# Third layer's edge loop: the 128 x 1024 destination compare as eight 128 x 128 compares with a per-partition scalar, in the accumulating form

## What is computed

```python
# h = relu(layernorm(x)); id_Xe = (src, dst)
features = H[id_Xe[0]]                               # a row per edge, by source node
M_in = concatenate([features, Xe], axis=1)           # Xe: 64 attributes per edge
Y = relu(M_in @ M_W.T + M_b)
Z = segment_sum(Y, id_Xe[1], num_segments=6250)      # sum over the edges of a destination
H_next = relu(concatenate([H, Z], axis=1) @ U_W.T + U_b)
x = x + H_next
```

## Time and profile before

| | |
|---|---|
| Time, median of 3 runs | 8234.38 us (8220.6 to 8267.23) |
| Profiled execution: span from first to last instruction | 6576.8 us |
| Profiled execution: its own time with what lies around the span | not recorded; the median less the span is 1657.6 us |
| PE, DVE, ACT, POOL busy, share of the span | 76%, 46%, 27%, 59% |
| The edge loop of the third layer, first to last gather issue on POOL | 3865.4 to 5915.4 us |
| In it: PE, DVE, ACT, POOL busy, of 2065 us | 1634, 360, 531, 1572 us |

### The profile page before, as it was taken

The page is one execution under the profiler, slowest core; times in us unless marked ns, Lnnn a source line. Parts: engine busy times, 40 slices in busy tenths (PEclk is TensorE's granted clock), DMA queues, the critical chain, the costliest instruction groups (busy, mean ns, idle before and its releaser), DMA issues. The chain is left out here.

```text
span 6576.8 us, 115590 instructions
## 1 busy us (share of the span) xinstructions
PE 5007.3 (76%) x35178; PEld 4266.4 (65%) x35178; DVE 3022.6 (46%) x3931; ACT 1799.8 (27%) x3844; POOL 3882.2 (59%) x3427
## 2 busy tenths in 40 slices
PE   2338888888888888841999957877878787771898
PEld 2315665665566655531999957777777777771898
DVE  7757777777777777746322131111111111113322
ACT  0024555555555545510000012222222222220000
POOL 5748788888788888750000047777777777773000
PEclk9668888888888888955999955555555555555898
DMA  9335555555555555522999846666666666652895
GB/s 358 77 84 141 151 153 152 143 150 150 154 155 146 150 149 154 153 61 84 329 366 366 312 128 202 204 203 203 205 204 203 206 204 197 202 178 62 336 389 215
DMA packets 659138, 1262.13 MB, mean 192 GB/s; under 512 B 167881, under 2 KB 467466, under 8 KB 633268
## 3 DMA queue, kind: packets, MB, share of 16 engines
q1 hardware_dynamic: 381076, 726.95, 32.8%
q10 hardware_dynamic: 168480, 416.21, 18.9%
q0 software_dynamic: 109184, 115.05, 9.8%
HBM read 924.66 MB, written 490.51 MB: 215 GB/s over the span
## 5 line engine op out<-in xcount | busy, mean ns | idle before, releaser
L696 POOL DMA_INDIRECT att_gl<-tab_l,att_ix x1568 | 1933.5, 1233 | 487.6 <-issue 472.3
L1184 POOL DMA_INDIRECT sum_gl<-tab_l,sum_ixs x1568 | 1572.3, 1003 | 524.7 <-issue 477.8
L937 ACT ACTIVATE att_acc<-att_pc 128x392 bf16<-128x392 f32 x2352 | 1083.3, 497 | 1324.1 <-PE att_pc L715 1122.6
L712 PE MATMUL att_pc<-att_ohl,att_ohv 128*128 128x392 bf16 x2352 | 863.0, 367 | 272.0 <-DVE att_ohl L812 271.7
L1134 PE MATMUL sum_pm<-sum_msg,sum_S 128*128 128x64 f32 x3136 | 680.0, 407 | 425.6 <-ACT sum_msg L1158 425.5
L1134 PEld LDWEIGHTS sum_pm<-sum_msg,sum_S 128*128 128x128 f32 x3136 | 647.0, 314 | 465.7 <-issue 264.7
L715 PE MATMUL att_pc<-att_acc,att_ohv 128*128 128x392 bf16 x2352 | 855.7, 364 | 116.3 <-ACT att_acc L937 112.7
L1104 DVE TENSOR_TENSOR sum_t<-sum_pb,sum_gl 128x512 f32<-128x512 f32 x196 | 135.6, 692 | 1692.1 <-DMA sum_gl<-tab_l,sum_ixs 1692.1
L1116 PE MATMUL sum_pb<-sum_wbs,sum_ea 64*128 64x64 f32 x3136 | 694.5, 419 | 27.4 <-DMA sum_ea<-in_ea64T 27.4
L731 PEld LDWEIGHTS att_pl<-att_xe,att_S 128*128 128x128 f32 x3136 | 599.3, 216 | 159.8 <-issue 137.3
L1116 PEld LDWEIGHTS sum_pb<-sum_wbs,sum_ea 64*128 64x128 f32 x3136 | 676.1, 329 | 39.0 <-DMA sum_ea<-in_ea64T 27.6
(11 more groups left out here) (360 smaller groups left out, 5190.2 us busy)
## 6 DMA issues: line engine op xcount, KB each, us to landing
A<-att_acc SPq DMA_DIRECT2D x2352, 98.0 KB
l_a<-A SPq DMA_DIRECT2D x147, 1568.0 KB, 9.2
l_at<-AT SPq DMA_DIRECT2D x98, 1568.0 KB
att_dall<-in_dst ACTq DMA_DIRECT2D x224, 448.0 KB
sum_dall<-in_dst SPq DMA_DIRECT2D x196, 512.0 KB, 4.8
sum_a<-A SPq DMA_DIRECT2D x49, 1568.0 KB, 10.1
AT<-sum_at ACTq DMA_DIRECT2D x49, 1568.0 KB, 5.4
tot<-att_o ACTq DMA_DIRECT2D x56, 1022.0 KB
```

Source lines behind the costliest of these rows:

```text
L696: nc.gpsimd.indirect_dma_start(out=gl[s][:, c, :], out_offset=None, in_=g.tab_l, in_offset=bass.IndirectOffsetOnAxis(ap=ix[s][:, c:c + 1], ...
L712: nc.tensor.matmul(pc[c][m % 2][:, 0:LO], ohv[c][h][:, m, :, 0], ohl[c][h][:, m // 2, :, m % 2], start=True, stop=False)
L937: nc.scalar.activation(acc[c][n % CR][:, :], pc[c][m % 2][:, 0:LO], ACT.Copy).then_inc(s_acc[c], 1)
L1184: nc.gpsimd.indirect_dma_start(out=gl[q][:, j, :], out_offset=None, in_=g.tab_l, in_offset=bass.IndirectOffsetOnAxis(ap=ixs[q][:, j:j + 1] ...
```

## The change

For each group, the one compare of 128 x 1024 becomes eight of 128 x 128. Each compares one chunk's destinations with one scalar per partition (this partition's edge's destination in that chunk), and adds 0. It is the form with `accum_out`, which also writes the sum over the line, here the number of edges of the chunk with this edge's destination, to a new tile `mult`. Nothing reads `mult`. The waits are the same, and stand before the first piece; the semaphore is raised by the last one.

```diff
@@ sum_chunks
         S = [st.sb(f"S{s}", [P, G, P]) for s in range(RB)]
+        mult = [st.sb(f"mult{s}", [P, G]) for s in range(RB)]
@@ DVE's body
                         wait_earlier(dve, s_mm[s], u)
                         dve.wait_ge(s_da[q], dt * 16 + 16)
-                        nc.vector.tensor_tensor(
-                            S[q][:, :, :], dall[q][:, :, :],
-                            spread(dst[:, bass.ds(c0, G)].unsqueeze(2), [P, G, P]), ALU.is_equal)\
-                            .then_inc(s_S[q], 1)
+                        for j in range(G):
+                            ins = nc.vector.tensor_scalar(S[q][:, j, :], dall[q][:, j, :], dst[:, bass.ds(c0 + j, 1)], 0.0,
+                                                          ALU.is_equal, ALU.add, accum_out=mult[q][:, j:j + 1])
+                        ins.then_inc(s_S[q], 1)
```

## The result

| | median, us | runs from and to |
|---|---|---|
| before | 8246.5 | 8220.6 to 8267.2 |
| after | 8617.8 | 8576.9 to 8681.9 |

The changed kernel is slower: after over before is 1.043, with an interval of 1.0365 to 1.0495. The prediction was 8147 us, in a range of 8110 to 8210.

The account below looks back on a forecast made before the run. The prediction took POOL's gather issues to bound the third layer's edge loop. Removing the 87.4 us for which the two-input compare held them, with the pieces priced at nothing, gave 8234.4 - 87.4 = 8147 us, range 8110 to 8210.

Parts of the forecast that it names:

- I take what lies around its span as it is, 1657.6 us.: Time outside the profiled span, assumed unchanged at 1657.6 us, so that the sum starts from the median, 8234.4 us.
- So POOL's gather issues set the pace, end to end.: Third layer's edge loop: POOL waits for nothing, and its issues take 10.46 us for each of 196 groups.
- The rival in which PE takes up the pace: Third layer's loop: PE's 1.6 us of room a unit runs out, half the gain is lost, 8190 us; chance 0.11.
- 87.4 us.: POOL's extra issue time in the third layer's loop, held by the two-input compare, 0.446 us each; forecast as the gain.
- The pieces' cost.: DVE's eight pieces a group: 0.286 us each, 2.3 to 4.0 us with sum write and register instruction, against 1.22 before.
- Does a piece hold POOL? I take nothing.: Whether DVE's one-SBUF-input pieces delay POOL's gather issues: bounds from nothing to all of POOL's work, taken as nothing.
- the first rival: Each DVE piece holds the start of a POOL issue; gain falls to 60 to 72 us, 8165 us; chance 0.14.
- Priced at nothing: DVE's 1.1 to 2.8 us more a group, taken as hidden behind its wait for gathers, shortest 4.91 us.
- The slower rival: DVE's pieces hold all of POOL's work, 1.82 us a group in place of 0.446: +270 us, 8504 us; chance 0.09.

Follow-up runs that it names:

- control: The kernel before, without any edit, timed and profiled again: 0.9993 of before, span 8403.5 us for a time of 8405.27 us.
- plain8: The kernel before with its compare as eight 128 x 128 pieces, scalar per partition, in the plain form without the accumulator: 1.0375 of before.
- fixed_col8: The kernel before with its compare as eight plain pieces, each reading a fixed column of dst instead of a register-addressed one (wrong chunks): 0.999 of before.
- longer_dve: The kernel before with an unread tensor_reduce of 128 x 1024 on DVE behind each compare: 0.9977 of before.
- half_gathers: The changed kernel with four gathers a group in place of eight, the add taking the four for all eight chunks: 0.9955 of before.
- pool_waits_pieces: The changed kernel with POOL also waiting, before a unit's gathers, for PE's transposes of two units before: 1.0065 of before.

## Why the prediction was wrong

- **"I take what lies around its span as it is, 1657.6 us."** This step failed, and with it the rest. Around a span lie 1.8 us, in before (`control`) and after. The difference was a difference between executions: the loop takes 2050 us in the one and 2462 us in the other, the first layer's loop 2410 and 3735. The number should have stopped me: 20% of the time outside of the first and last instruction has nothing in the profile to fill it.
- **"So POOL's gather issues set the pace, end to end."** True of the profile that was read. In the timed executions POOL waits 452 us for the add before the change, and 866 us after it. The rival in which PE takes up the pace had named the engine, with 0.11 and at most the loss of the gain; it was priced from PE's modelled durations (16.8 us a unit), which hold no late signal. In the second profile of before a unit takes 25.2 us from one first bias matmul to the next, and after the change 28.7 us (means).
- **"87.4 us."** The mechanism was right: the longest issue went from 1.913 to 0.961 us and POOL's busy time from 1534.1 to 1479.2 us. The size in the timed kind is 54.9 us, 0.28 us a group. All of it was given back, since an engine that waits 452 us gains nothing from shorter work.
- **The pieces' cost.** A little under the bounds: a compare takes 0.341 us, where I took 0.286, but the next starts 0.26 to 0.27 us after it, and the read of the accumulator, 0.082 us, is hidden. A group takes 2.21 us against 2.3 to 4.0. The register instruction is hidden, since pieces with and without it both take 1.65 us (`plain8`, `fixed_col8`).
- **"Does a piece hold POOL? I take nothing."** Right for the accumulating form. The plain form held 120 of 1568 issues a little, up to 1.070 us: the first rival, told for the accumulating form. The Trainium skill, "SBUF — State Buffer", section "Who interferes with whom", says that the accumulating form is never in two-port mode, and the accumulating rows agree: of 1568 issues beside 1568 pieces the longest took 0.961 us.
- **"Priced at nothing", of DVE's time.** Right as to time (`longer_dve`). Wrong that nothing else could come of it: with the pieces the stretch in which PE's signals are late falls behind the adds, in the transposes (8 units of 97, then 79), and POOL waits 414 us more.
- **The slower rival** (8504 us) had the sign and, by luck, most of the size (270 us of some 370): no issue was held for the length of a piece.

**What is shown and what is not.** Shown: the loop is long where the transposes' signals are late, the cost goes away with three of four transposes, and it goes away with one more wait of POOL; in both cases the lateness is before the adds again. Shown too: ahead of the adds, and in the crawl of `half_gathers`, it is PE's signals that are late, and not its work. That POOL's gathering is the cause rests on the ends of the stretches in before and in `half_gathers`, and on `pool_waits_pieces`; in after most ends do not show it. Not shown: by what means the signals are held (many of these waits name no releaser but "remote"), whether the cause is POOL's issuing or the traffic of its gathers, whether in the crawl of after PE's work is late too, why all this is absent in the first profile, where POOL gathers without a pause as well, why the stretch begins 3 us after POOL in one case and later in the other, and what in eight pieces tips it, since four pieces, fixed columns and equal time do not. The granted clock is 0.50 to 0.52, the lower of its two levels, in all of these loops, the quick one too, so the clock is not the difference.

## What to carry to other kernels

Before reasoning from a profile, hold its span against the timed runs: if they are 20% apart, it is of another execution, and its pacemaker need not be yours. In a ring of engines that run ahead of each other, look at which event stops the one that disturbs the others: here a wait that looks like pure cost gave 3.5% back. When a consumer waits long for an engine, look at whether several signals of that engine come together: then its work was done, and what is late is the signal. And take a small gain where it is small: the compare in two halves, 0.9949 (0.9921 to 0.9976), is the best of the versions that leave no work out, and half a per cent is near what such runs can tell.

## What the hardware did that I had not expected

- TensorE's semaphore updates came up to 15 us behind its modelled rows. Before the change the updates for two groups of eight fp32 matmuls, 3.41 us apart when on time, came 0.16 us apart, together with those for up to three batches of transposes. After the change the copies that wait for four 128 x 128 bf16 transposes came 2.9 to 4.3 us apart, against 0.43 in PE's rows.
- In before and in `half_gathers` these stretches ended some 3 to 4 us after the start of POOL's last indirect DMA. In the changed kernel most ended while POOL was still issuing.
- The accumulating tensor_scalar of 128 x 128 lasts 0.341 us and starts every 0.265; the plain one, the two-input one and the fixed-column one all need about 0.21 us apiece.
- Two 512-element two-input compares hold POOL less than one of 1024: its busy time in the loop is 1502.4 us against 1534.1, the longest issue 1.286 us against 1.913. The loop was 40 us shorter, on another chip.
